# A fused macaron block on one core: one run a partition for the router weights, a reordered prologue, an fp32 left half of the first expert call, and routing weights that are never multiplied out

## The reference

```
x = x + 0.5 * ffn(layernorm(x))
x = x + mlp(layernorm(x))
x = x + 0.5 * ffn(layernorm(x))

ffn(x):  scores = x @ Wr.T                        # 64 experts
         gates  = softmax of the 16 highest scores, 0 for the other experts
         h      = x @ A.T                         # 64 experts x rank 16 = 1024 columns
         out    = 2 * ((h * gate of its expert) @ B)
mlp(x):  s = silu(x @ Wg.T); in each row the 688 smallest |s| of 1376 are set to 0
         out = (s * (x @ Wu.T)) @ Wd.T
```

## Time and profile before

| | us |
|---|---|
| median of 3 runs | 705.83 (705.51 to 705.92) |
| profiled execution | 706.07 |
| its span | 704.3 |
| PE busy | 689.8 (98%) |
| DVE busy | 471.7 (67%) |
| ACT busy | 359.6 (51%) |
| POOL busy | 217.9 (31%) |

### The profile page before, as it was taken

How to read it: one execution, slowest core, us unless ns; L and a number is a source line. 1 busy time by engine, 2 the same in 40 slices (tenths; PEclk the granted TensorE clock), 3 DMA queues, 4 the chain that set the end, 5 groups by cost and what they waited for, 6 DMA issues and landing times.

```text
span 704.3 us, 10405 instructions
## 1 busy us (share of the span) xinstructions
PE 689.8 (98%) x3699; PEld 333.9 (47%) x3699; DVE 471.7 (67%) x984; ACT 359.6 (51%) x467; POOL 217.9 (31%) x545
## 2 busy tenths in 40 slices
PE   4999999999999999999999999999999999999998
PEld 3444444444444444544445444444444444444445
DVE  6899776866585666647666576566746565738863
ACT  5788876525545253462525545254453445676210
POOL 4122435424324042341423315142240424444000
PEclk9999999999999999999999999999999999999999
DMA  9977414245434162543414434242442415123453
GB/s 323 290 194 204 63 16 87 51 81 102 77 72 97 38 96 52 99 77 50 98 30 102 75 66 89 45 95 45 87 76 34 84 30 102 31 56 72 77 93 82
DMA packets 171867, 62.28 MB, mean 88 GB/s; under 512 B 163648, under 2 KB 163904, under 8 KB 171808
## 3 DMA queue, kind: packets, MB, share of 16 engines
q1 hardware_dynamic: 171808, 61.56, 41.7%
HBM read 16.97 MB, written 4.19 MB: 30 GB/s over the span
## 4 chain that ended last, share of the span: by engine, by line
PE 74%; POOL 7%; ACT 6%; issue 5%; DVE 5%; DMA 2%; SPq 0%; DVEq 0%; POOLq 0%; ACTq 0%
PE ps L616 14%; PE ps L617 14%; PE ps L618 14%; PE ps L733 10%; PE ps L737 10%; PE ps L734 10%; ACT signs L967 5%; POOL small L535 2%; POOL small L532 2%; POOL small L531 1%; DMA mem<-w_a 1%; POOL small L533 1%; DMA xt_f<-halves 1%; DVE mem L1356 1%; DVE tops L1358 1%
## 5 line engine op out<-in xcount | busy, mean ns | idle before, releaser
L967 ACT ACTIVATE signs<-mem,small 128x1376 bf16<-128x1376 f32 x112 | 161.4, 1441 | 152.9 <-POOL small L535 135.6
L616 PE MATMUL ps<-w_a_hi,xt_f 128*128 128x512 f16 x248 | 94.0, 379 | 0.0
L618 PE MATMUL ps<-w_a_lo,xt_f 128*128 128x512 f16 x248 | 94.0, 379 | 0.0
L734 PE MATMUL ps<-w_b_lo,pt_hi 128*128 128x512 f16 x248 | 94.0, 379 | 0.0
L617 PE MATMUL ps<-w_a_hi,xt_f 128*128 128x512 f16 x248 | 94.0, 379 | 0.0
L733 PE MATMUL ps<-w_b_hi,pt_hi 128*128 128x512 f16 x248 | 94.0, 379 | 0.0
L491 POOL TENSOR_SCALAR rvar<-mv 128x1 f32<-128x1 f32 x48 | 11.4, 238 | 186.6 <-DVE mv L1211 185.1
L616 PE MATMUL ps<-w_g_hi,xt 128*128 128x512 f16 (+1 forms) x192 | 68.5, 357 | 0.2 <-DVE mem L1327 0.2
L618 PE MATMUL ps<-w_g_lo,xt 128*128 128x512 f16 (+1 forms) x192 | 68.5, 357 | 0.0
L617 PE MATMUL ps<-w_g_hi,xt 128*128 128x512 f16 (+1 forms) x192 | 68.5, 357 | 0.0
L618 PE MATMUL ps<-w_u_lo,xt 128*128 128x512 f16 (+1 forms) x192 | 68.5, 357 | 0.0
(11 more groups left out here) (152 smaller groups left out, 1225.1 us busy)
## 6 DMA issues: line engine op xcount, KB each, us to landing
x<-x SPq DMA_DIRECT2D x14, 256.0 KB, 3.4
out<-x SPq DMA_DIRECT2D x13, 256.0 KB, 2.3
mem<-w_g SPq DMA_DIRECT2D x4, 688.0 KB, 12.5
mem<-w_u SPq DMA_DIRECT2D x4, 688.0 KB, 5.6
mem<-w_d SPq DMA_DIRECT2D x5, 512.0 KB, 6.2
mem<-w_a SPq DMA_DIRECT2D x4, 512.0 KB, 6.1
mem<-w_b SPq DMA_DIRECT2D x4, 512.0 KB, 9.0
pt_hi<-p_hi SPq DMA_TRANSPOSE x32, 3.2
```

What stands on the lines that cost most here:

```text
L616: pe.matmul(dst, x_hi, w_hi, start=start, stop=False)
L618: return pe.matmul(dst, x_hi, w_lo, start=False, stop=stop)
L734: pe.matmul(dst, x_hi[:, c, :], lo[m.name][:, c, :], start=False, stop=False)
L967: act.activation(signs[:, :], mags[h], ACT.Sign, bias=thr[h], scale=-1.0, accum_out=bal[h]).then_inc(counted[h], 1)
```

## The change

1. `w_r` is laid out so that each partition's 256 values are one run of 1 KB in memory; before they were four runs of 256 B. It is loaded by one plain DMA.
2. `route` no longer writes `weight`. `apply_route` multiplies h by `chosen` and by the scalar `inv_total` in one instruction, and the factor GATE_S moves into `p_to_hi` (as the scale of the activation) and `p_to_lo` (as the scalar).
3. In call 0 the left half of h (columns 0 to 511) is made by four fp32 matmuls, from the unsplit, unscaled w_a and an fp32 copy of the transposed x (`x_whole`, kept in `routed`). `experts_begun` makes only the right half. `apply_route_first` gives the left half its own factor, inv_total times the scale of w_a.
4. The filler matmuls move from call 0 (16 of them) to the start of PE's work (24 of them). The norm sums of w_a go to bank 2.
5. The order of the prologue changes on all engines, as the diff shows.

```diff
@@ SP
+                    if m is MR:
+                        sp.dma_start(mem[:, m.at:m.at + DC * KE], dram["r"]
+                                     ).then_inc(w_loaded["r"][0], 16)
+                        continue
...
             load_x(3)
-            load_w(MG, 0, 1, 2, 3)
-            load_x(4)
+            load_w(MG, 0, 1)
             turn_x(1, 2)
-            load_u(0)
+            load_w(MG, 2)
             turn_p_hi(0)
             turn_x(1, 3)
+            load_w(MG, 3)
+            turn_p_lo(0)
+            load_x(4)
+            load_u(0)
+            turn_p_hi(1)
             load_u(1)
-            turn_p_lo(0)
+            load_x(5)
+            turn_p_lo(1)
             load_u(2)
-            turn_p_hi(1)
-            load_x(5)
             load_x(6)
-            turn_p_lo(1)
             load_u(3)
@@ POOL
+            aim(0)
             rstd(2, 2)
-            aim(0)
+            search(0, 0)
             make_scale(MD)
-            search(0, 0)
@@ PE
+            def experts_whole(*chunks):
+                for c in chunks:
+                    pe.wait_ge(w_loaded["a"][c], 16)
+                    pe.matmul(bank(EXP), x_whole[:, c, :], staged(MA, c, 1, P)[:, 0, 0:BANK],
+                              start=c == 0, stop=c == DC - 1)
...
-                    busy(16)
                     mm = experts_begun(e, x_hi, x_lo, turn_of)
...
+            pe.wait_ge(const_made, 1)
+            busy(24)
+            norms(MR)
             pe.wait_ge(const_made, 4)
-            norms(MR)
             turn(0)
-            norms(MA)
+            norms(MA, 0, 2)
+            pe.wait_ge(x_whole_ready, 1)
+            experts_whole(0)
+            norms(MA, 2, 3)
+            experts_whole(1)
+            norms(MA, 3)
+            experts_whole(2, 3)
             experts(1, 0, fresh=True, turn_of=1)
...
             combine(1, 1)
+            experts(1, 4)
             pe.wait_ge(scale_made, 4)
             norms(MU)
-            experts(1, 4)
@@ ACT
+            def turned_whole():
+                act.wait_ge(turned, 1)
+                act.activation(x_whole, bank(DOWN).rearrange("p (c t) -> p c t", c=DC), ACT.Copy
+                               ).then_inc(x_whole_ready, 1)
...
             square(MR, 0)
             square(MA, 0)
+            square(MA, 1)
+            turned_whole()
+            square(MA, 2)
+            square(MA, 3)
             turned_to_hi(0)
             split_hi(MR, 0)
-            for n in range(1, len(MA.pieces)):
-                square(MA, n)
...
             tanh(0)
-            p_to_hi(4)
             square(MD, 3)
             square(MD, 4)
             magnitude(0)
+            p_to_hi(4)
@@ DVE
-                link(dve.tensor_scalar(weight[:, :], chosen[:, :], inv_total, GATE_S,
-                                       ALU.mult, ALU.mult))
...
-                dve.tensor_tensor(
-                    routed[:, :].rearrange("p (k r) -> p k r", r=RANK),
-                    bank(banks_of(k), KR).rearrange("p (k r) -> p k r", r=RANK),
-                    weight[:, :].unsqueeze(2).to_broadcast([P, KE, RANK]),
-                    ALU.mult).then_inc(routed_ready, 1)
+                dve.scalar_tensor_tensor(
+                    out=routed[:, :].rearrange("p (k r) -> p k r", r=RANK),
+                    in0=bank(banks_of(k), KR).rearrange("p (k r) -> p k r", r=RANK),
+                    scalar=inv_total, in1=chosen[:, :].unsqueeze(2).to_broadcast([P, KE, RANK]),
+                    op0=ALU.mult, op1=ALU.mult).then_inc(routed_ready, 1)
...
+                dve.scalar_tensor_tensor(out=p_lo[:, :], in0=routed[:, :], scalar=GATE_S,
+                                         in1=p_hi[:, :], op0=ALU.mult, op1=ALU.subtract
...
             read_norm(MR)
             square_right(0)
-            turned_to_lo(0)
-            split_lo(MR, 0)
             square_right(1)
-            make_unscale(unscale_r, "r")
             square_right(2)
             square_right(3)
             read_norm(MA)
+            turned_to_lo(0)
             norm_stats(1, 1)
+            split_lo(MR, 0)
+            make_unscale(unscale_r, "r")
+            norm_stats(1, 2)
             read_scores(0)
-            norm_stats(1, 2)
+            norm_apply(1, 1)
             split_lo(MA, 0)
-            norm_apply(1, 1)
             split_lo(MA, 1)
             split_lo(MA, 2)
+            turned_to_lo(1)
+            split_lo(MA, 3)
             norm_apply(1, 2)
-            split_lo(MA, 3)
-            turned_to_lo(1)
+            choose(0)
             x_to_lo(1, 2)
-            choose(0)
...
-            apply_route(0)
+            apply_route_first()
...
             p_to_lo(2)
+            read_norm(MG)
             x_to_lo(1, 4)
             add_ffn(1, 0)
             norm_stats(2, 0)
-            read_norm(MG)
```

More of the change, by code:

```diff
@@ L72, in build @@
     N, D = x.shape
-    KE, KR, I = w_r.shape[1], w_a.shape[1], w_g.shape[1]
+    KE, KR, I = w_r.shape[1] * P // w_a.shape[0], w_a.shape[1], w_g.shape[1]
     RANK = KR // KE
@@ L950, in p_to_hi @@
                     act.wait_ge(pt_hi_loaded, 16 * k)
-                act.activation(p_hi[:, :], routed[:, :], ACT.Copy).then_inc(p_hi_ready, 1)
+                act.activation(p_hi[:, :], routed[:, :], ACT.Copy, scale=GATE_S).then_inc(p_hi_ready, 1)
             def p_to_hi_last():
@@ L957, in p_to_hi_last @@
                 act.wait_ge(pt_hi_loaded, 16 * k)
[L958 removed]
+                act.activation(p_hi[:, 0:BANK], routed[:, 0:BANK], ACT.Copy, scale=GATE_S)
                 act.wait_ge(routed_ready, k + 1)
[L960 to L961 removed]
+                act.activation(p_hi[:, BANK:KR], routed[:, BANK:KR], ACT.Copy,
+                               scale=GATE_S).then_inc(p_hi_ready, 1)
             def count(t, n):
@@ L1023, in _ @@
             square(MB, 0)
+            square(MB, 1)
             x_to_hi(1, 2)
-            for n in range(1, len(MB.pieces)):
-                square(MB, n)
+            square(MB, 2)
+            square(MB, 3)
             exps(0)
@@ L1043, in _ @@
             x_to_hi(1, 4)
-            for n in range(len(MU.pieces)):
-                square(MU, n)
+            square(MU, 0)
+            square(MU, 1)
             split_hi(MG, 0)
+            square(MU, 2)
+            p_to_hi(3)
             split_hi(MG, 1)
-            p_to_hi(3)
+            square(MU, 3)
             x_to_hi(2, 0)
@@ L1279, in apply_route_last, with apply_route_first @@
                     dve.wait_ge(of, at)
-                    dve.tensor_tensor(
-                        routed[:, halves_of[h]].rearrange("p (k r) -> p k r", r=RANK),
-                        bank(banks_of(k) + h).rearrange("p (k r) -> p k r", r=RANK),
-                        weight[:, heads[h]].unsqueeze(2).to_broadcast([P, KE // 2, RANK]),
-                        ALU.mult).then_inc(done, 1)
+                    dve.scalar_tensor_tensor(
+                        out=routed[:, halves_of[h]].rearrange("p (k r) -> p k r", r=RANK),
+                        in0=bank(banks_of(k) + h).rearrange("p (k r) -> p k r", r=RANK),
+                        scalar=inv_total,
+                        in1=chosen[:, heads[h]].unsqueeze(2).to_broadcast([P, KE // 2, RANK]),
+                        op0=ALU.mult, op1=ALU.mult).then_inc(done, 1)
+            def apply_route_first():
+                link(dve.tensor_scalar(inv_unscaled, inv_total, scale["a"], None, ALU.mult))
+                dve.wait_ge(expert_done, 1)
+                for h, factor in enumerate((inv_unscaled, inv_total)):
+                    mm = dve.scalar_tensor_tensor(
+                        out=routed[:, h * BANK:(h + 1) * BANK].rearrange("p (k r) -> p k r", r=RANK),
+                        in0=bank(EXP + h).rearrange("p (k r) -> p k r", r=RANK), scalar=factor,
+                        in1=chosen[:, h * KE // 2:(h + 1) * KE // 2].unsqueeze(2).to_broadcast(
+                            [P, KE // 2, RANK]),
+                        op0=ALU.mult, op1=ALU.mult)
+                mm.then_inc(routed_ready, 1)
             def p_to_lo(k):
@@ L1533, in _ @@
             add_ffn(1, 1)
+            read_norm(MU)
             norm_stats(2, 1)
@@ L1709 @@
         "x": x.reshape(B * S, D),
-        "w_r": np.ascontiguousarray(np.transpose(inputs["L0_ffn_Wr"])),
+        "w_r": np.ascontiguousarray(np.transpose(np.transpose(inputs["L0_ffn_Wr"]).reshape(
+            D // P, P, K), (1, 0, 2)).reshape(P, D // P * K)),
         "w_a": np.ascontiguousarray(np.transpose(np.reshape(a, (K * R, D)))),
```

41 lines of the change are left out of this document (19 added, 22 removed).

## The result

The changed kernel took 709.79 us (median of 4 runs, 709.47 to 711.67), the kernel before 705.67 in the same job: ratio 1.0058, 95% interval 1.004 to 1.0077. The forecast was 704.8 and its range ended at 707.0: it was wrong, in sign too. The profiled execution took 709.47.

The account below looks back on a forecast made before the run. TensorE bounds the kernel, busy 689.8 of 704.3 us, so only an earlier matmul train counts. Terms -1.0 (T), -0.29 (routing), +0.3 (new waits) make -1.0: 705.1 profiled, 704.8 median; eight-in-ten range 703.4 to 707.0.

Parts of the forecast that it names:

- T: Start of tile 2's first score matmul on TensorE, from which matmuls run as a train; 27.51 us in the kernel before.
- the wait at 640: TensorE's wait of 0.47 us at 640.0, forecast to lose up to 0.29 us through the routing change.
- Which pitch holds: Clock level of the early fp32 matmuls on TensorE: slow or fast about equally likely, fast a little ahead.
- rival B: Slow pitch holds until w_a's norm: norm read at 12.65, T 27.6, total 705.8; chance 0.20.
- What can be late anew: Transposes of tiles 3 and 4 landing late, margins 0 to 0.5 us: +0.3 us together, bounds 0 and 1.5.
- T gains 1.0 us: Prologue: tile 2's transpose wait goes and VectorE is late next, so T comes at 26.5 for 27.51.
- Routing weights: One 255 ns VectorE multiply fewer in each of 32 calls; on the path in one, gaining up to 0.29 us.
- rival E: The product of PSUM, pointer scalar and broadcast weight runs at half rate: 706.6 to 707.5; chance 0.05.
- w_r: One run a partition in the prologue load: 0.2 us off everything landing after it, bounds 0 and 0.36.
- Fillers in front: 24 filler matmuls at TensorE's start take 2.6 us inside its 4.6 us of idle: free.
- Rival C: Fp32 matmuls of chunks 2 and 3 delay tile 0's scores, which VectorE awaits: 706.8, or 707.6; chance 0.17.
- D: Upside: no new wait, and the waits at 106.6 and 133.7 go as well: 703.8; chance 0.18.

Follow-up runs that it names:

- e9: The changed kernel with SyncE's (SP's) whole prologue order put back to that of the kernel before: 707.00 us, ratio 1.0018 against before.
- e1: The changed kernel with x of tile 4 loaded right behind the first two w_g pieces, ahead of tile 2's transpose: 708.22 us, ratio 1.0036.
- e8: e7 with 24 more filler matmuls while w_a lands: 709.82 us, ratio 1.006 against before.
- e16: e1 with VectorE's read of w_g's norm put back behind the low half of tile 4's x: 708.3 us, ratio 1.0052.
- e7: e1 with loads of w_u and x moved away from the transposes of tile 1's p_lo and tile 4's x: 711.19 us, ratio 1.0077.
- e2: The changed kernel without the fp32 left half, both halves of call 0 made in f16, all orders kept: 709.75 us, ratio 1.0061.
- e6: The kernel before with w_g pieces 2 and 3 behind tile 2's transpose and x of tile 4 ahead of it: 707.18 us, ratio 1.0023.
- e14: The kernel before with w_r in one run a partition and one w_g piece moved behind tile 2's transpose: 704.47 us, ratio 0.9997.
- e12: e9 with the 24 more filler matmuls of e8: 707.63 us, ratio 1.0024 against before.
- e4: The kernel before with the new routing product alone, weights never multiplied out: 706.27 us, ratio 1.0012.

## Why the prediction was wrong

The terms side by side, forecast and then changed's profile: T -1.0 and +0.60; new waits behind it +0.3 and +2.79 (w_b 0.47, tile 4's transpose 2.32); the wait at 640 -0.29 and -0.31. The sum was to be -1.0 and is +3.1 of the 3.4 us.

**Which pitch holds: the slow one.** This was left open with the fast one a little ahead; rival B had its mechanism. A chunk took 1.9 us against 1.71 at the slow pitch, and about 1.0 against 0.86 at the fast one. The norm read came at 13.27 (B: 12.65) and T at 28.11 (B: 27.6). In before T was held by the transpose 1.2 us behind the VectorE strand, so a norm 1.8 us later moved T by only 0.6. Four f16 products per chunk, put as the upper end, were nearly right (4.4 to 4.6 measured); the pitch was read from where the clock had risen in before (16.1), which says nothing of fillers followed by gaps. In e9 the column shows it. PE and stretches of e9_sp_old:

```profile
6.04 0.63 PE L674 MATMUL ps<-xt,normed 128*128 128x128 f32 x4 [1.55 <-DVE normed L1247]
...
8.47 2.07 PE L681 MATMUL ps<-mem,routed 128*128 128x512 f32 x2 [0.27 <-ACT routed L956]
```

```profile
6.00:8.00 2.00, 0.84 (x7) 0.55 (x7) 1.33 (x4) 1.44 (x5) 1.77 (x3) 0.84 1.02 414
8.00:10.00 2.00, 1.73 (x4) 0.77 (x5) 0.90 (x3) 1.34 (x4) 0.00 (x0) 0.50 1.03 405
...
14.00:16.00 2.00, 2.00 (x18) 0.80 (x17) 1.86 (x7) 2.00 (x3) 1.18 (x4) 0.96 1.06 389
```

The 24 fillers did raise the clock there (the four transposes at 6.04 take 0.63 us, 1.11 in the earlier trace rows); but TensorE had 0.2 us of work in the two us from 4, and the clock was down when the fp32 work came. In changed's own trace the transposes were slow as well (1.09 us). Of the eleven profiles with the 24 fillers in front four have fast transposes (e1, e8, e9, e16), of the seven without them none.

**What can be late anew: the step that failed.** It was put at 0.3 us, with an upper bound of 1.5; undoing the SP order gives back 2.8 us (e9). Two things were missed. x of tile 4, which stood ahead of the first transpose, was moved behind four of them, and the working never asked who waits for it: VectorE stood 2.04 us for it. Moving it back is worth 1.6 us (e1). And the landing of tile 4's transpose was entered as 3.2 us; the 6.6 us of tile 2's in before served only for the upper bound. Three transposes of p in before's trace, also with loads issued shortly ahead, took 4.8, 5.7 and 5.9 us. In changed the two on the chain took 4.42 and 4.49 us, tile 4's in e1 5.31, p_lo's in e7 6.64. The bound of 1.5 us was no bound, since it took one late transpose, not a chain of three DMAs. Taking the two norms' order for the risk was at most half right: e16's one profile has 0.4 us less wait without it, the median has nothing.

**T gains 1.0 us.** Without the fp32 half, or with the queue's part alone, T does come at 26.4 to 26.6 (e2, 26.41; e6, 26.55; e14, 26.49). But "what the new prologue is worth is how much sooner that train starts" doesn't hold: T came 1.0 us sooner in e6 and 1.7 in e2, experts of tile 1 ended 1.9 us sooner in e12, and none was faster. The transposes of tiles 2, 3 and 4 and the halves of w_b hang on the queue as well, so an earlier train runs into them. Only in e14's profile was the gain at T kept to the end, and its median isn't shown to be faster.

**Routing weights.** The step at 640 was right, forecast -0.29 and measured -0.31, and the product took 1.28 us as sized: rival E falls. Missed was the tail: GpSimd's steps stretched beside VectorE's two-input instructions, at most 0.67 us in the time of e4. Changed itself has no such wait at 660.

**w_r.** 0.2 us sooner itself, as sized, but the last w_a piece landed at 10.45 as before: the gain doesn't travel. **Fillers in front** were free, as put. **Rival C** had the right sign and a wrong place: scores were read at 16.2, low halves of w_a followed without idling for them; the price came at tile 4. C had a chance of 0.17 and ended at 707.6; the time, 709.8, was above every rival's.

Two readings in the working were off without weight for the outcome: of the "4.4 us in pieces" ahead of 28 us, 1.3 were a wait for tile 0's normalized x, not for w_a, and D's own terms give 703.7, not 703.8.

## What to carry to other kernels

When a load is moved behind transposes in an in-order queue, write down who reads it and when, for every load moved, and price each landing by the slowest row with loads ahead of it, not by the quiet ones. A train of matmuls that starts sooner gains only what every DMA-fed stage behind it can follow; look for the next two or three before booking it. Move one piece at a time: with one w_g piece behind the transpose no later transpose was late (e14), with two the gain was more than given back (e6). And compare one profile's waits with that run's own time, not with the median.

## What the runs showed of the hardware

- A wait of 2.71 us amid dense work was followed by 3.4 us at the 1.2 GHz level (granted clock 0.52 and 0.63 in two stretches of e2), which cost 1.7 us on top, and one of 2.48 us by 3.0 us (e7), which cost 1.5; after one of 2.32 us (changed) the clock stayed.
- The column of the granted clock read 1.00 in changed between 8 and 14 us while fp32 chunks took 1.9 us and in e9 read 0.50 for the same: the pitch between starts is the sounder reading.
- An fp32 matmul of 512 columns costs some 1.0 us at the fast and 1.9 at the slow pitch, 4.4 to 4.6 f16 ones (0.216 and 0.427).
- GpSimd's 0.34 us step took 1.80 to 1.82 us in the four traces in which it started 0.05 to 0.06 us before a VectorE product of two SBUF tensors.
- A transposing DMA of this prologue landed 3.0 to 3.3 us after its issue at best. Those that took longer (up to 7.6 us, e1) had loads issued shortly ahead of them, but a w_g piece issued 3.1 us ahead slowed p_hi's of tile 0 in changed hardly at all (3.3 us).
